# Variances on three partition groups, so that the merge's small matmuls use row groups of TensorE

## The chip, the cores and the metric

The program runs on one core of one Trainium2 chip. The metric is the time of one execution on the device in microseconds (us), the median of several runs.

## The reference, cut to what matters

The input is 8 images of 64 x 64 positions with 96 channels. Four layers follow each other, each adding its result to its input:

```python
x = x + L0(_gn(x), ...)      # cross kind
x = x + L1(_gn(x), ...)      # snake kind
x = x + L2(_gn(x), ...)      # cross kind
x = x + L3(_gn(x), ...)      # causal kind, one direction, no layer norm
```

Inside a layer the channels are projected to 192, convolved and gated, and a state-space recurrence runs over the positions in four directions (in L3 in one). What matters here is how layers 0 to 2 end, for every position, over its 192 channels:

```python
y = out[:, 0] + inv[:, 0] + wh + invwh          # the four directions, plus Ds * xs
mu = y.mean(-1, keepdims=True)
var = y.var(-1, keepdims=True)
y = (y - mu) * rsqrt(var + 1e-05) * ln_gamma + ln_beta
y = y * silu(z)
return y @ out_proj_w.T                          # 192 -> 96
```

## The kernel before

`build` runs, for each of the four layers, `expand_stage`, `scan_stage` and `merge_stage`, one after the other, each as a block with its own program for every engine. The images are worked on in pairs, four pairs in all. The 192 channels of two images are 384 rows, laid on the 128 partitions as three tiles (`TILES`): tile 0 holds the first 128 channels of image 0, tile 2 those of image 1, and tile 1 the last 64 channels of both, image 0 on partitions 0 to 63 and image 1 on 64 to 127. An image has 4,096 positions, worked on in eight banks (`NB`) of 512 columns.

`merge_stage` (lines 1137 to 1505) does two things at once. In each bank of pair p it also takes three of the 24 jobs that sum the directions of pair p + 1: SyncE (SP) loads `ya`, `yb` and, for a row job, `ub` (512 KB each) into one of three slots; GpSimd (POOL) adds ya and yb (`pair_up`, L1483); VectorE (DVE) adds them to `total` (`add_job`: L1427 a row job, L1438 a column job, which in the snake kind is two instructions of half the size). Jobs come as four row jobs and four column jobs, three times over.

The bank itself, in a normalized layer, goes through these steps, with semaphores between the engines:

- `centre` (L1287, TensorE, PE): 7 matmuls of 128 x 128 on 512 columns subtract the mean and leave the centred values in `cent`.
- `square` (L1365) and `take` (L1370, both ScalarE, ACT): the squares go to `sq`, a copy to `tn`.
- `variance` (L1297, PE): 3 matmuls with the 2-column table `average_by` sum the squares of both images into two partitions of `scale[:, 0, :]`.
- `deviation` (L1376, ACT): square root into `root`, 2 partitions by 512.
- reciprocal (L1462, DVE), in place in `root`.
- `spread` (L1305, PE): 3 matmuls, one for each tile, with the 2-row table `spread_by` carry 1/deviation from the two partitions to all 128, into the three banks of `scale`.
- product (L1467, DVE) of `tn` and `scale`; `gain` (L1382, ACT); gate by `zc` (L1504, POOL).
- `project` (PE): for each image b one matmul on the 128 rows of its own tile (L1318) and one on its 64 rows of tile 1 (L1320), added up in bank b of `outp`.
- `residual` (L1209, DVE) adds `outp` to `xr`, which SP loaded (L1258) and stores after the last bank (L1268).

The order is written out by hand. On PE a bank is `variance(c)`, `centre(c + 1)`, `spread(c)`, `project(c - 1)`:

```python
variance(p, c)
if c + 1 < NB:
    centre(p, c + 1, half)
spread(p, c)
if c:
    project(p, c - 1)
```

On DVE it is the reciprocal, one job, the product, the bank's two other jobs, `residual(c - 1)`. On ACT it is the root, `square(c + 1)`, `gain(c)`, `take(c + 1)`. On POOL it is three `pair_up`, then the gate. `variance` waits for the squares and for the product of the bank before; `spread` for the reciprocal; `project` for the gate and for the residual of the bank before it; SP's loads of a job wait until DVE is done with the job three before, and its load of `xr` for the store of the last pair. The causal layer has no variance, no spread and its own branch in `project`.

Of the kernel before, what the change touches and what calls it, by code (L numbers as in the profile page):

```python
# [22 lines left out]
ACT = mybir.ActivationFunctionType  # L23

P = 128
# [1111 lines left out]
def merge_stage(nc, kind, T, W, useq, yseq, zgate, x_t, out, last):  # L1137
# [27 lines left out]
    with ExitStack() as ctx:  # L1165
# [4 lines left out]
        def sb(name, shape, dt=F32):  # L1170
            return ctx.enter_context(nc.sbuf_tensor(name + W["tag"], shape, dt))
# [10 lines left out]
        average_by = sb("average_by", [P, TILES, 2])  # L1182
        spread_by = sb("spread_by", [2, TILES, P])
        zc = [sb(f"zc{j}", [P, TILES, BANK]) for j in range(2)]
        sq = sb("sq", [P, TILES, BANK]) if norm else None
        root = sb("root", [2, BANK])
# [25 lines left out]
        with nc.Block() as block:  # L1212
# [65 lines left out]
            def _(pe):  # L1278
# [13 lines left out]
                def variance(p, c):  # L1292
                    pe.wait_ge(sem["squared"], p * NB + (c + 1))

                    pe.wait_ge(sem["normed"], p * NB + (c + 1))
                    for s in range(TILES):
                        mm = pe.matmul(scale[0:2, 0, :], average_by[:, s, :], sq[:, s, :], start=(s == 0),  # L1297
                                       stop=(s == TILES - 1))
                    mm.then_inc(sem["var_full"], 1)

                def spread(p, c):

                    pe.wait_ge(sem["inverted"], p * NB + (c + 1))
                    for s in range(TILES):
                        mm = pe.matmul(scale[:, s, :], spread_by[:, s, :], root[:, :], start=True, stop=True)  # L1305
                    mm.then_inc(sem["spread"], 1)

                def project(p, c):
# [6 lines left out]
                    for b in range(2):  # L1315
                        rows = slice(64 * b, 64 * b + 64)
                        if not last:
                            pe.matmul(outp[0:DM, b, :], wo[:, 2 * b * DM:(2 * b + 1) * DM], g[:, 2 * b, :],  # L1318
                                      start=True, stop=False)
                            mm = pe.matmul(outp[0:DM, b, :], wo[rows, DM:2 * DM], g[rows, 1, :],  # L1320
                                           start=False, stop=True)
                        else:
# [37 lines left out]
            def _(act):  # L1360
# [11 lines left out]
                def deviation(p, c):  # L1372
# [3 lines left out]
                    act.activation(root[:], scale[0:2, 0, :], ACT.Sqrt, bias=T["eps"][0:2, 0:1])\  # L1376
# [192 lines left out]
def constants():  # L1569
# [9 lines left out]
    for b in range(2):  # L1579
        for n in range(NS):  # L1580
            pick[:, b, n, b, n // QUADS, n % QUADS] = one
    group = np.kron(np.eye(DM // 3), np.ones((3, 3))) / 3
# [5 lines left out]
        "average": (np.stack([batch == 0, batch == 1], axis=-1) / DI).astype(np.float32),  # L1588
        "spread": np.stack([batch.T == 0, batch.T == 1]).astype(np.float32),
# [68 lines left out]
```

## Time and profile before

| | |
|---|---|
| median of 3 runs | 39,340.68 us (39,318.74 to 39,354.67) |
| the profiled execution, its own time | 39,340.42 us |
| its span, first to last instruction | 39,338.6 us |
| mean granted TensorE clock | 0.754 of full speed |
| instructions | 330,119 |

The profile is of one execution. "Busy" is the time an engine spent in instructions; a matmul in f32 is recorded as two passes over its columns, so counts of PE are twice those of the program. PEld is the load of weights, which overlaps PE. The granted clock is 1.00 for 2.4 GHz and 0.50 for 1.2 GHz. In a timeline consecutive instructions of one kind are merged into a row with their count (x14), and the last bracket tells how long the engine had idled and which instruction released it. "Cross", "snake" and "causal" are the kinds of the layers.

### The profile page before, as it was taken

What the parts mean: (1) busy time and instruction counts of PE and PEld (TensorE: products, weight loads), DVE (VectorE), ACT (ScalarE), POOL (GpSimd) and SP (SyncE); (2) the same over time, 40 slices, a digit from 0 to 9 for tenths busy, and PEclk for the clock granted to TensorE, in tenths of its full rate; (3) what the DMA queues carried; (4) which work ended last, traced back from release to release, by engine and by line L of the source; (5) the groups of instructions that cost most, each with busy time, mean ns of one, the idle gap of its engine ahead of it and who ended that gap; (6) DMA issues with size and microseconds to landing.
All of it is one profiled execution on the core that took longest, in us unless ns stands there. A gap on an engine that the chain in (4) does not pass through costs nothing. (4 is left out here: it accounts for less than half of the span.)

```text
span 39338.6 us, 330119 instructions
## 1 busy us (share of the span) xinstructions
PE 27496.9 (70%) x73952; PEld 7178.8 (18%) x73952; DVE 34763.5 (88%) x18992; ACT 18062.4 (46%) x22589; POOL 33220.1 (84%) x7824
## 2 busy tenths in 40 slices
PE   3777777777774777777777774777777777775777
PEld 1111111111111111111111111111111111111114
DVE  6999999999957999999999967999999999965994
ACT  2555555555522554554555522545455454523451
POOL 1999999999962999999999952999999999963994
PEclk6777777777766777777777766777777777777775
DMA  4666666666664666666666664666666666665665
GB/s 132 160 160 157 161 160 161 158 162 160 160 213 146 158 161 159 162 159 159 157 161 161 161 212 145 159 159 157 160 160 159 159 157 160 161 209 162 158 157 174
DMA packets 2388645, 6388.13 MB, mean 162 GB/s; under 512 B 692056, under 2 KB 835936, under 8 KB 2376032
## 3 DMA queue, kind: packets, MB, share of 16 engines
q1 hardware_dynamic: 2387040, 6374.58, 62.7%
q14 instruction: 1556, 12.75, 0.1%
q8 instruction: 49, 0.80, 0.0%
HBM read 2973.68 MB, written 764.47 MB: 95 GB/s over the span
## 5 line engine op out<-in xcount | busy, mean ns | idle before, releaser
L1100 POOL TENSOR_TENSOR h<-h,c 128x2048 f32<-128x2048 f32 x4992 | 22509.1, 4525 | 1278.4 <-ACT state L959 1274.3
L901 DVE TENSOR_TENSOR_SCAN h<-decay,state,slot 128x1024 f32<-128x1024 f32 x6656 | 15615.9, 2346 | 681.1 <-ACT state L1047 20.1
L809 PE MATMUL psy<-h,t_fold 128*32 128x512 f32 x40000 | 12230.6, 787 | 265.6 <-ACT ybuf L1020 265.6
L744 PE MATMUL slot<-bc,pick 96*128 96x512 bf16 x13328 | 5060.7, 477 | 8763.4 <-DVE h L897 5512.5
L877 DVE TENSOR_TENSOR slot<-du,slot 128x1024 f32<-128x1024 f32 x6656 | 8050.7, 1210 | 1039.3 <-PE slot L744 945.0
L951 ACT ACTIVATE decay<-delta,na 128x1024 f32<-128x1024 f32 x6664 | 7583.2, 1146 | 2332.2 <-DVE h L901 2158.6
L897 DVE TENSOR_TENSOR_SCAN h<-slot,state,made 128x1024 f32<-128x1024 f32 x3328 | 7624.6, 2326 | 15.5 <-ACT slot L951 15.5
L1120 POOL TENSOR_TENSOR made<-du,b 128x2048 f32<-128x2048 f32 x1664 | 7524.6, 4522 | 127.1 <-DMA b<-bcdram 123.4
L951 ACT ACTIVATE slot<-delta,na 128x1024 f32<-128x1024 f32 x3328 | 3716.6, 1117 | 6481.4 <-DVE h L901 6476.4
L809 PEld LDWEIGHTS psy<-h,t_fold 128*32 128x32 f32 x40000 | 2244.1, 131 | 8523.9 <-issue 8231.2
L744 PEld LDWEIGHTS slot<-bc,pick 96*128 96x128 bf16 x13328 | 908.9, 104 | 14839.8 <-DVE h L897 8044.3
L959 ACT COPY state<-h 128x2 f32<-128x2 f32 x4992 | 925.8, 185 | 3762.3 <-DVE h L901 2769.4
L1112 POOL TENSOR_TENSOR du<-delta,u 128x1024 f32<-128x1024 f32 x628 | 1483.6, 2362 | 929.0 <-ACT delta L998 929.0
L762 PE MATMUL psc<-dts,wdt 32*128 32x512 f32 x2512 | 1977.6, 893 | 0.9 <-ACT dts L1031 0.9
L441 POOL COPY us<-us 128x4096 f32<-128x4096 f32 (+1 forms) x48 | 359.0, 7494 | 1913.4 <-ACT us L359 1913.4
L1483 POOL TENSOR_TENSOR ya<-ya,yb 128x1024 f32<-128x1024 f32 x360 | 1030.7, 2873 | 793.4 <-DMA ub<-useq 740.2
L777 PE MATMUL psc<-relu,t_ident 128*128 128x512 f32 x2512 | 1658.8, 795 | 22.8 <-DVE excess L908 22.8
L422 DVE SCALAR_TENSOR_TENSOR acc<-xp,convw,acc 128x4096 f32<-128x4096 f32 x312 | 1560.1, 5000 | 11.2
L998 ACT COPY delta<-psc 128x1024 f32<-128x1024 f32 x628 | 635.5, 1012 | 1989.5 <-PE psc L777 1989.5
L752 PE MATMUL psc<-u,wx 128*96 128x512 f32 x2544 | 1482.1, 683 | 30.6 <-DMA bdt<-in_bdt 29.8
L777 PE MATMUL psc<-log,t_ident 128*128 128x512 f32 x2512 | 1326.3, 624 | 0.0
L777 PE MATMUL psc<-excess,t_less 128*128 128x512 f32 x2512 | 1179.7, 592 | 0.0
(103 smaller groups left out, 17260.9 us busy)
## 6 DMA issues: line engine op xcount, KB each, us to landing
delta<-delta SPq DMA_DIRECT2D x10048, 128.0 KB, 2.8
du<-du SPq DMA_DIRECT2D x10048, 128.0 KB, 2.9
c<-bcdram SPq DMA_DIRECT2D x6720, 128.0 KB, 2.8
b<-bcdram SPq DMA_DIRECT2D x6688, 128.0 KB, 3.0
u<-useq SPq DMA_DIRECT2D x212, 1536.0 KB, 6.6
yseq<-ybuf SPq DMA_DIRECT2D x624, 512.0 KB, 2.7
ya<-yseq SPq DMA_DIRECT2D x420, 512.0 KB, 4.3
yb<-yseq SPq DMA_DIRECT2D x360, 512.0 KB, 5.1
```

The lines of the kernel that those rows point to most:

```text
L422: dve.scalar_tensor_tensor(out=a, in0=src, scalar=w, in1=a, op0=ALU.mult, op1=ALU.add).then_inc(sem["conv_step"], 1)
L744: mm = pe.matmul(slot[s % 2][:, cols], pick[:, rows_of, :], bc[q % 2][:, cols], start=True, stop=True)
L762: pe.matmul(psc[:, HALF[a]], wdt[q][:, t, :], dts[q][:, HALF[a]], start=True, stop=True)\
L777: mm = pe.matmul(psc[:, HALF[a]], T["less" if term == 2 else "ident"][:, :], (relu, log, excess)[term][:, HALF[a]], start=(term == 0), sto ...
L809: mm = pe.matmul(psy[rows, cols], T["fold"][:, :], h[v % H_RING][:, c, cols], start=(v % QUADS == 0), stop=(v % QUADS == QUADS - 1), skip_ ...
L877: dve.tensor_tensor(slot[s % 2][:], du4[j % DU_RING][:, s % 2, :], slot[s % 2][:], ALU.mult)\
L897: dve.tensor_tensor_scan(out, slot[s % 2][:, order], made[p % MADE_RING][:, s % 2, order], first, ALU.mult, ALU.add).then_inc(sem["h_ready ...
L901: dve.tensor_tensor_scan(out, decay[s % DECAY_RING][:, order], slot[s % 2][:, order], first, ALU.mult, ALU.add).then_inc(sem["h_ready"], 1)
L951: act.activation(dst[:], delta4[j % DELTA_RING][:, s % 2, :], ACT.Exp, scale=na[q][:, k:k + 1])\
L1100: pool.tensor_tensor(both[:], both[:], c4[g][:].unsqueeze(1).broadcast_to((P, 2, CH)), ALU.mult)\
L1112: pool.tensor_tensor(du[:], delta[:], u[q][:, t, :], ALU.mult).then_inc(sem["du_ready"], 1)
L1120: pool.tensor_tensor(made[k % MADE_RING][:], du4[j % DU_RING][:], b4[k % B_RING][:].unsqueeze(1).broadcast_to((P, 2, CH)), ALU.mult)\
```

## The change

Three tables and the code around them change. `average_by` has 96 columns instead of 2: columns 0 and 1, 32 and 33, 64 and 65 hold the same two averages and the rest are zero, so the variances of the two images come out three times, on partitions 0, 32 and 64. `root` has 96 partitions, and the root and the reciprocal work on all of them. `spread_by` is one table of 96 x 128, in which rows 32s and 32s + 1 serve tile s; the matmul for tile s reads its weights and its moving data from those two partitions. In `project`, outside the last layer, the two matmuls of 128 rows now come first and the two of 64 rows (partitions 0 to 63 and 64 to 127) after them.

```diff
--- before.py
+++ after.py
@@ -1179,11 +1179,12 @@
         dsum = sb("dsum", [P, TILES])
         lng, lnb = (sb(n, [P, TILES]) for n in ("lng", "lnb"))
         centre_by = sb("centre_by", [P, TILES, TILES, P])
-        average_by = sb("average_by", [P, TILES, 2])
-        spread_by = sb("spread_by", [2, TILES, P])
+
+        average_by = sb("average_by", [P, TILES, 96])
+        spread_by = sb("spread_by", [96, P])
         zc = [sb(f"zc{j}", [P, TILES, BANK]) for j in range(2)]
         sq = sb("sq", [P, TILES, BANK]) if norm else None
-        root = sb("root", [2, BANK])
+        root = sb("root", [96, BANK])
         tn = [sb(f"tn{j}", [P, TILES, BANK]) for j in range(2)]
         ob = sb("ob", [P, 2, 4, DM]) if last else None
         cent = ctx.enter_context(nc.psum_tensor("cent" + W["tag"], [P, TILES, BANK], F32))
@@ -1294,15 +1295,17 @@
 
                     pe.wait_ge(sem["normed"], p * NB + (c + 1))
                     for s in range(TILES):
-                        mm = pe.matmul(scale[0:2, 0, :], average_by[:, s, :], sq[:, s, :], start=(s == 0),
+                        mm = pe.matmul(scale[0:96, 0, :], average_by[:, s, :], sq[:, s, :], start=(s == 0),
                                        stop=(s == TILES - 1))
                     mm.then_inc(sem["var_full"], 1)
 
                 def spread(p, c):
 
                     pe.wait_ge(sem["inverted"], p * NB + (c + 1))
+
                     for s in range(TILES):
-                        mm = pe.matmul(scale[:, s, :], spread_by[:, s, :], root[:, :], start=True, stop=True)
+                        rows = slice(32 * s, 32 * s + 2)
+                        mm = pe.matmul(scale[:, s, :], spread_by[rows, :], root[rows, :], start=True, stop=True)
                     mm.then_inc(sem["spread"], 1)
 
                 def project(p, c):
@@ -1312,14 +1315,18 @@
                     if last and c == 0:
                         pe.wait_ge(sem["x_in"], p * 16 + 16)
                     g = tn[c % 2]
-                    for b in range(2):
-                        rows = slice(64 * b, 64 * b + 64)
-                        if not last:
+                    if not last:
+                        for b in range(2):
                             pe.matmul(outp[0:DM, b, :], wo[:, 2 * b * DM:(2 * b + 1) * DM], g[:, 2 * b, :],
                                       start=True, stop=False)
+
+                        for b in range(2):
+                            rows = slice(64 * b, 64 * b + 64)
                             mm = pe.matmul(outp[0:DM, b, :], wo[rows, DM:2 * DM], g[rows, 1, :],
                                            start=False, stop=True)
-                        else:
+                    else:
+                        for b in range(2):
+                            rows = slice(64 * b, 64 * b + 64)
                             for j in range(4):
                                 o = outp[:, b, j * DM:(j + 1) * DM]
                                 tok = slice(j * P, (j + 1) * P)
@@ -1373,7 +1380,7 @@
 
                     act.wait_ge(sem["spread"], p * NB + (c + 1))
                     act.wait_ge(sem["var_full"], p * NB + (c + 2))
-                    act.activation(root[:], scale[0:2, 0, :], ACT.Sqrt, bias=T["eps"][0:2, 0:1])\
+                    act.activation(root[:], scale[0:96, 0, :], ACT.Sqrt, bias=T["eps"][0:96, 0:1])\
                         .then_inc(sem["rooted"], 1)
 
                 def gain(p, c):
@@ -1579,14 +1586,19 @@
     for b in range(2):
         for n in range(NS):
             pick[:, b, n, b, n // QUADS, n % QUADS] = one
+    average, spread = np.zeros((P, TILES, 96)), np.zeros((96, P))
+    for s in range(TILES):
+        for b in range(2):
+            average[:, :, 32 * s + b] = (batch == b) / DI
+            spread[32 * s + b] = batch[:, s] == b
     group = np.kron(np.eye(DM // 3), np.ones((3, 3))) / 3
     return {
         "ident": np.eye(P, dtype=np.float32),
         "pick": pick.reshape(96, 2 * QUADS, P),
         "fold": np.tile(np.eye(GROUP, dtype=np.float32), (QUADS, 1)),
         "group": group.astype(np.float32),
-        "average": (np.stack([batch == 0, batch == 1], axis=-1) / DI).astype(np.float32),
-        "spread": np.stack([batch.T == 0, batch.T == 1]).astype(np.float32),
+        "average": average.astype(np.float32),
+        "spread": spread.astype(np.float32),
         "centre": (eye - same / DI).astype(np.float32),
     }
```

The order of instructions changes on PE alone, in two places. The first is a steady bank of a merge: the spread (L1305 before, L1308 now) and the projection behind it. `outp<-tn_0,wo` is a matmul of the projection. Before:

```order
L1287 MATMUL cent<-total_0,centre_by 128x512 x7
L1305 MATMUL scale<-root,spread_by 128x512 x3
L1318 MATMUL outp<-tn_0,wo 96x512
L1320 MATMUL outp<-tn_0,wo 96x512
L1318 MATMUL outp<-tn_0,wo 96x512
L1320 MATMUL outp<-tn_0,wo 96x512
L1297 MATMUL scale<-sq,average_by 2x512 x3
```

Now:

```order
L1288 MATMUL cent<-total_0,centre_by 128x512 x7
L1308 MATMUL scale<-root,spread_by 128x512 x3
L1320 MATMUL outp<-tn_0,wo 96x512 x2
L1325 MATMUL outp<-tn_0,wo 96x512 x2
L1298 MATMUL scale<-sq,average_by 96x512 x3
```

The matmul of 64 rows of image 0 (L1320 before, L1325 now) has moved behind the matmul of 128 rows of image 1 (L1318 before, L1320 now), and stands next to its twin.

The second is the end of a pair, where two projections follow the last spread (REGISTER_ALU prepares a semaphore's value). Before:

```order
L1305 MATMUL scale<-root,spread_by 128x512 x3
L1309 REGISTER_ALU
L1318 MATMUL outp<-tn_0,wo 96x512
L1320 MATMUL outp<-tn_0,wo 96x512
L1318 MATMUL outp<-tn_0,wo 96x512
L1320 MATMUL outp<-tn_0,wo 96x512
L1309 REGISTER_ALU
L1318 MATMUL outp<-tn_0,wo 96x512
L1320 MATMUL outp<-tn_0,wo 96x512
L1318 MATMUL outp<-tn_0,wo 96x512
L1320 MATMUL outp<-tn_0,wo 96x512
```

Now:

```order
L1308 MATMUL scale<-root,spread_by 128x512 x3
L1312 REGISTER_ALU
L1320 MATMUL outp<-tn_0,wo 96x512 x2
L1325 MATMUL outp<-tn_0,wo 96x512 x2
L1312 REGISTER_ALU
L1320 MATMUL outp<-tn_0,wo 96x512 x2
L1325 MATMUL outp<-tn_0,wo 96x512 x2
```

Both projections are regrouped in the same way; what stands before and behind them is as it was.

## Rows read from the trace of the kernel before

**Rows 1.** The page, part 1: busy us of each engine, share of the span, instructions.
```profile
PE 27496.9 (70%) x73952; PEld 7178.8 (18%) x73952; DVE 34763.5 (88%) x18992; ACT 18062.4 (46%) x22589; POOL 33220.1 (84%) x7824
```

**Rows 2.** Table by stretch: us, each engine's busy time (instructions), clock, DMA share, GB/s.
```profile
11050.00:11980.00 930.00, 701.03 (x1088) 191.61 (x1088) 462.67 (x249) 189.23 (x196) 473.21 (x152) 0.68 0.64 225
22850.00:23800.00 950.00, 701.37 (x1088) 190.94 (x1088) 533.67 (x375) 190.50 (x197) 460.39 (x152) 0.67 0.64 223
```

**Rows 3.** Timeline of PE, one steady bank: start us, us, engine, line, operation.
```profile
11220.50 6.28 PE L1287 MATMUL cent<-total,centre_by 128*128 128x512 f32 x14
11226.70 2.84 PE L1305 MATMUL scale<-root,spread_by 2*128 2x512 f32 x6
11229.47 1.22 PE L1318 MATMUL outp<-tn,wo 128*96 128x512 f32 x2
11230.62 2.02 PE L1320 MATMUL outp<-tn,wo 64*96 64x512 f32 x2
...
11236.48 4.75 PE L1297 MATMUL scale<-sq,average_by 128*2 128x512 f32 x6
```

**Rows 4.** Timeline of DVE: the reciprocals that bound the intervals, one product.
```profile
11200.68 3.34 DVE L1462 RECIPROCAL root<-root 2x512 f32<-2x512 f32 x1 [3.70 <-ACT root L1376]
...
11229.65 1.75 DVE L1467 TENSOR_TENSOR tn<-tn,scale 128x1536 f32<-128x1536 f32 x1 [2.75 <-PE scale L1305]
...
11324.65 3.34 DVE L1462 RECIPROCAL root<-root 2x512 f32<-2x512 f32 x1 [3.48 <-ACT root L1376]
...
11422.70 3.33 DVE L1462 RECIPROCAL root<-root 2x512 f32<-2x512 f32 x1
...
11528.28 3.34 DVE L1462 RECIPROCAL root<-root 2x512 f32<-2x512 f32 x1 [4.63 <-ACT root L1376]
```

**Rows 5.** Table by stretch, columns as in rows 2: granted clock and DMA.
```profile
11220.50:11226.70 6.20, 6.20 (x15) 2.57 (x14) 5.32 (x2) 0.68 (x1) 3.99 (x3) 1.00 0.93 359
11226.70:11229.47 2.77, 2.77 (x7) 1.03 (x6) 0.20 (x1) 1.45 (x1) 2.29 (x1) 1.00 0.51 160
11230.70:11236.40 5.70, 5.70 (x6) 1.10 (x6) 4.19 (x3) 2.23 (x3) 2.57 (x1) 0.50 0.59 201
11236.50:11241.10 4.60, 4.60 (x7) 0.57 (x6) 1.28 (x2) 1.44 (x1) 4.02 (x3) 0.56 1.01 395
11362.30:11365.00 2.70, 2.68 (x7) 0.44 (x7) 0.00 (x0) 1.30 (x1) 0.00 (x0) 1.00 0.59 206
11023.60:11027.30 3.70, 3.68 (x17) 0.64 (x16) 3.60 (x3) 1.09 (x1) 3.70 (x2) 0.50 1.04 240
11168.00:11325.00 157.00, 150.41 (x250) 41.88 (x250) 82.58 (x49) 46.45 (x47) 88.46 (x30) 0.76 0.70 244
```

**Rows 6.** Timeline of the scan before the merge: the fold on PE.
```profile
11023.63 3.66 PE L809 MATMUL psy<-h,t_fold 128*32 128x512 f32 x16
```

**Rows 7.** Groups by line and shape: count, busy us, mean ns, idle before.
```profile
L1438 DVE TENSOR_TENSOR total<-total,ya 128x1024 f32<-128x1024 f32 x120 | 361.2, 3010 | 36.5 <-POOL ya L1483 32.0
L1438 DVE TENSOR_TENSOR total<-total,ya 128x512 f32<-128x512 f32 x120 | 240.4, 2003 | 14.4 <-POOL ya L1483 11.0
L1427 DVE SCALAR_TENSOR_TENSOR total<-ub,dsum,ya 128x1024 f32<-128x1024 f32 x240 | 336.3, 1411 | 864.3 <-DMA ub<-useq 519.2 <-POOL ya L1483 345.2
L1462 DVE RECIPROCAL root<-root 2x512 f32<-2x512 f32 x96 | 320.4, 3338 | 407.1 <-ACT root L1376 407.1
L1209 DVE TENSOR_TENSOR xr<-xr,outp 96x512 f32<-96x512 f32 x128 | 81.7, 676 | 156.7 <-PE outp L1320 156.7
L1320 PEld LDWEIGHTS outp<-tn,wo 64*96 64x96 f32 x384 | 74.7, 254 | 278.7 <-issue 278.7
```

**Rows 8.** Timeline of PE and DVE at the end of the first pair.
```profile
11328.04 5.49 PE L1305 MATMUL scale<-root,spread_by 2*128 2x512 f32 x6 [4.20 <-DVE root L1462]
...
11335.31 7.96 DVE L1438 TENSOR_TENSOR total<-total,ya 128x1024 f32<-128x1024 f32 x2
...
11352.30 8.40 PE L1287 MATMUL cent<-total,centre_by 128*128 128x512 f32 x14
```

## The prediction

> **What bounds it now.** The page first [rows 1]: over the whole run VectorE (DVE) is busy 88%, GpSimd (POOL) 84%, TensorE (PE) 70%. Those shares belong to the scan, which the change leaves alone; only the three normalized merges are touched. A table by stretch [rows 2] shows the first (cross) and the second (snake), 930 and 950 us long: PE is busy 701 us in both, VectorE only 463 and 534, GpSimd 473 and 460. The third is of the first's kind. Together they are about 2,800 us, 7% of the run, and a gain can come from nowhere else.
>
> Next, one steady bank on PE [rows 3]. By the starts, the centring takes 6.20 (11220.50 to 11226.70), the spread 2.77, and the projection of the bank before 7.01: four matmuls, the first 1.15 to the next one's start, so the other three 5.86 / 3 = 1.95 each. VectorE's reciprocals give the beat [rows 4]: six intervals from 11200.68 to 11324.65 are 20.66 us each, and in the second pair five from 11422.70 to 11528.28 are 21.1. The variance is then 20.66 less the other three, 4.68, and nothing is left for a gap on PE. A first pair of a merge has six such intervals and each of the other three has five, 21 per merge, 63 in all. In them PE is the bound.
>
> Then the clock [rows 5]. The centring and the spread are granted 1.00 (2.4 GHz). The clock falls right behind the spread, which streams only 2 of 128 rows for 2.77 us; the rest of the projection is granted 0.50 (1.2 GHz), and so is nearly all of the variance (0.56). It is back when the centring begins, after full-height variances. Where PE went from a centring straight to a variance, that variance had 1.00 and took 2.67 us.
>
> **The change, part by part.** Every f32 matmul is recorded as two passes, so the spread's 3 matmuls are 6 passes (x6 in the row).
>
> 1. *Spread.* Its three matmuls now sit in row groups 0, 32 and 64 and write different banks. No row of the kernel shows row groups side by side. The ends are: nothing gained (6 rounds, 2.77), or all at once (2 rounds, 2.77 - 4 x 0.44 = 1.0; 0.44 is the centring's 6.20 / 14 passes). The nearest row is the scan's fold with 32-column weights in different column groups [rows 6]: 16 passes took 3.66 us while the clock was 0.50 [rows 5], about 0.9 us per round of four; one after another they would take 16 x 0.9 = 14. I take 1.0, saving 1.77.
>
> 2. *Projection.* The two half-height matmuls now follow each other, in rows 0 to 63 and 64 to 127, into different banks. By the same row I let them run together: three steps, not four, saving 1.95 in the low clock; the other end is 0. At full clock a step is at most 1.15 (the first matmul in rows 3), three are 3.45.
>
> The Trainium skill, "TensorE: Matmul & The Clock Gate", in its part on packing small matmuls, says that matmuls start and end strictly in program order. By that rule the second pass of one matmul would hold the next one back: spread 4 rounds, the two halves 3 passes long, 0.9 and 0.9 us dearer. The fold's row speaks against it: in strict order only the second pass of one and the first of the next could overlap, 8 rounds or 7 us, where 3.66 was measured.
>
> 3. *Variance.* 96 weight columns, not 2. A load of 96 columns is 254 ns [rows 7], under the pass before it (0.44 or more). Cost 0; if that cover is gone, 6 x 0.25 = 1.5 us a bank. The pass itself should not change: at full clock one with 2 weight columns (variance, 2.67 / 6) and one with 128 (centring) both take 0.44.
>
> 4. *Square root and reciprocal* take 512 elements per partition on 96 partitions, not 2. VectorE's product on 128 partitions by 1,536 takes 1.75 and the reciprocal on 2 by 512 takes 3.34 [rows 4, 7]: the partitions clearly do not set the time. I count nothing; were the reciprocal half as long again, VectorE's banks would grow by 1.7 and the gain fall by a third. ScalarE (ACT) is busy 46 of 157 us [rows 5] and could take twice the root.
>
> 5. *Loads.* The two tables grow by some 190 KB a merge: 4 merges times 0.5 us at the 359 GB/s of the centring in rows 5, +2 us.
>
> **The steady bank after it.** In the clock as now: 20.66 - 1.77 - 1.95 = 16.9. With the clock high all through: 6.20 + 1.0 + 3.45 + 2.67 = 13.3. I take the clock as mostly high, since what preceded each fall, the long 2-row stretch, shrinks to 1 us and the halves are paired to full height. Then PE is no longer the bound, and others are:
>
> - DMA: busy share 0.70 of 157 us in the first pair's eight banks (the stretch holds 7.6) [rows 5]: 110 / 7.6 = 14.5 us a bank.
> - VectorE: reciprocal 3.34, product 1.75, residual 2 x 0.68, together 6.44, and three jobs: a row job is 1.41, a column job 3.01 in the cross kind and 2 x 2.00 in the snake kind [rows 7]. The five steady banks hold 2, 0, 3, 1, 1 column jobs: cross 13.9, 10.7, 15.5, 12.3, 12.3; snake 15.9, 10.7, 18.5, 13.3, 13.3.
>
> The larger of DMA and VectorE bank by bank averages 14.7 (cross) and 15.6 (snake). To both I add 0.8 for hand-overs (an estimate: four a bank of about 0.2, as from the spread's end at 11229.47 in rows 3 to the product at 11229.65 in rows 4), since these engines now wait for one another. So 15.5 and 16.4, against 20.66: 42 x 5.15 + 21 x 4.25 = 306 us.
>
> **The pair ends.** Here the clock is low and one chain counts [rows 8]: spread at 11328.04 (5.49, 0.9 a pass), product, two jobs that hold VectorE 7.96, residual, last projection, next centring at 11352.30. The spread becomes 1.9 (-3.6) and the projection three steps (-1.95): 5.5 for each of 12 pair ends, 66 us. Between the last reciprocal of this pair and the third of the next lie 98 us in three intervals [rows 4]; behind the pair end they wait for the residual's 3 MB store and load and for jobs. For the last two of them I count 0, and keep 3.5 us each, one low spread (18 of them, 63 us), for the lower end.
>
> **Sum.** 306 + 66 - 2 = 370 us. The profiled execution took 39,340.4 us (span 39,338.6), a hair below the median of 39,340.7: **38,970 us**, 0.94% less. About 0.2% (80 us) is what a measurement of this kernel can tell from no change.
>
> **Rivals.**
>
> *A. The clock keeps its two halves.* For it: the projection and the variance ran low although PE had no gap. Against: the spread before each fall is cut to a third. Interval 16.9 (only the snake's bank of 18.5 is above): 63 x 3.7 + 66 = 299, giving 39,040. Chance 0.18.
>
> *B. Passes in strict order, or no overlap at all.* Strict order at high clock makes the PE bank 13.3 + 1.8 = 15.1, still under 15.5, and a pair end saves 2.8, so 306 + 34: 39,000; with the clock of rival A it is 18.7, 123 + 34: 39,180. No overlap leaves two fewer changes of matmul height a bank, some 0.12 us each (1.95 against 5.49 / 3), 96 x 0.24 = 23: 39,320, no change. Chance 0.06 for strict order, 0.06 for none.
>
> *C. Slower: the clock stays low through the centring.* Row-group matmuls use few rows, and shorter variances leave PE waiting for VectorE, so the clock might not rise before the centring. A bank all low: 2 x 6.20 + 1.9 + 3 x 1.95 + 2 x 2.67 = 25.5, or 4.8 over today; 63 x 4.8 - 66 = 236 slower: 39,580. The sign turns where the bank passes 20.66 by more than a pair end's saving, at about (20.66 - 13.3) / (25.5 - 13.3) = 60% of the way to all low. For: pair ends where the spread ran low throughout. Against: the clock rises today after a variance that ran low. Chance 0.05.
>
> **Numbers.** Forecast 0.65, A 0.18, B 0.12, C 0.05. Low end: no hand-over cost (14.7 and 15.6, 357 us) plus 66 and 63: 486 less, 38,854, taken as 38,840. High end: past A, to strict order in the low clock, cut at 39,150. Left out are no overlap, C and tails. Faster by over 0.2%: 0.65 + 0.18 + 0.06 and a little lost to tails, 0.89; the same 0.06; slower 0.05.
>
> **What would show it.** Right: the spread's six passes take about 1.0 us at full clock, three starts within 0.05 us; the two half-height matmuls start together; the projection takes 3.5 us or less; steady reciprocals stand 14 to 19 us apart, unevenly, longest where three column jobs fall; PE waits for VectorE; granted clock of the first pair's 157 us above 0.76. Wrong: an even beat of 17 (A), six spread passes one by one at 0.44 (B), centrings of 12 us (C), a reciprocal or root that takes longer than 3.34 or 0.8 us, or PE loads that show between the variance's passes.

## The result and the profile after

The changed kernel takes 38,959.85 us (median of 4 runs, 38,956.73 to 39,009.38) against 39,329.71 us before in the same measurement: 370 us less, a ratio of 0.9906 with a 95% interval of [0.9893, 0.9918]. It is faster. The profiled execution of the changed kernel has a span of 38,961.1 us.

The page, part 1, of the changed kernel (busy us, share of the span, instructions), beside [rows 1]:

```profile
PE 26823.7 (69%) x73952; PEld 7089.6 (18%) x73952; DVE 34963.4 (90%) x18992; ACT 18056.2 (46%) x22589; POOL 33194.7 (85%) x7824
```

PE lost 673 us of busy time with the same number of instructions. VectorE gained 200 us, though it was given no more work: its jobs take longer, of which more below.

The timeline of PE in the changed kernel, two banks of the first pair (start us, us, line, operation; compare [rows 3]):

```profile
11247.08 1.75 PE L1308 MATMUL scale<-root,spread_by 2*128 2x512 f32 x6 [2.86 <-DVE root L1469]
11248.76 3.73 PE L1320 MATMUL outp<-tn,wo 128*96 128x512 f32 x4
11252.42 2.01 PE L1325 MATMUL outp<-tn,wo 64*96 64x512 f32 x4
11254.36 2.81 PE L1298 MATMUL scale<-sq,average_by 128*96 128x512 f32 x6
11257.02 6.17 PE L1288 MATMUL cent<-total,centre_by 128*128 128x512 f32 x14
11263.28 1.13 PE L1308 MATMUL scale<-root,spread_by 2*128 2x512 f32 x6
11264.34 1.96 PE L1320 MATMUL outp<-tn,wo 128*96 128x512 f32 x4
11266.23 1.10 PE L1325 MATMUL outp<-tn,wo 64*96 64x512 f32 x4
11267.26 2.81 PE L1298 MATMUL scale<-sq,average_by 128*96 128x512 f32 x6
```

The second bank is the forecast to the letter: the spread's six passes are over in 1.06 us (11263.28 to 11264.34), where [rows 3] had 2.77; the two half-height matmuls (four passes) take 1.03 us, the time of one; projection 2.92 and variance 2.7 (from 4.68), all at full clock. Taken one by one, the first passes of its three spread matmuls start 0.007 us apart (11263.277, .284, .291), and so do the second ones (.811, .817, .824). The first bank is of another kind: PE waited 2.86 us for the reciprocal, and the projection behind it ran low (3.66 and 1.94 us). Both kinds are common. In 33 of the 63 steady banks the projection ran below full clock: in none of the 18 in which PE had waited less than 0.5 us before the spread, in 32 of the 36 in which it had waited over 1.5 us. The table by stretch says the same of the two banks, and gives the first pair's steady banks (us; busy PE, PEld, DVE, ACT, POOL; clock, DMA share, GB/s; for the kernel before see [rows 5]):

```profile
11248.80:11254.30 5.50, 5.50 (x11) 1.32 (x8) 5.40 (x4) 2.23 (x3) 3.57 (x2) 0.50 0.65 245
11263.30:11270.00 6.70, 6.70 (x20) 2.00 (x20) 6.70 (x3) 4.31 (x5) 2.98 (x2) 1.00 0.96 322
11184.00:11293.00 109.00, 90.37 (x222) 31.23 (x220) 99.45 (x47) 39.62 (x42) 82.37 (x26) 0.92 0.82 290
```

For the kernel before, that last stretch reads:

```profile
11184.00:11293.00 109.00, 106.99 (x184) 30.34 (x182) 66.75 (x36) 32.09 (x33) 62.37 (x20) 0.78 0.69 242
```

PE was full (107 of 109 us) and is not any more; the clock went from 0.78 to 0.92. (A fixed stretch catches other banks in each execution: the changed kernel's second profile has 0.86 in the same one. Over all 63 steady intervals the two profiles agree, 0.901 and 0.906, against 0.725 before.)

The reciprocals on VectorE after the change, answering to [rows 4]: six intervals from the first of these rows to the second, five from the third to the fourth.

```profile
11194.75 3.35 DVE L1469 RECIPROCAL root<-root 96x512 f32<-96x512 f32 x1 [3.04 <-ACT root L1383]
...
11293.05 3.34 DVE L1469 RECIPROCAL root<-root 96x512 f32<-96x512 f32 x1
...
11384.12 3.33 DVE L1469 RECIPROCAL root<-root 96x512 f32<-96x512 f32 x1
...
11461.43 3.33 DVE L1469 RECIPROCAL root<-root 96x512 f32<-96x512 f32 x1
```

That is 16.4 and 15.5 us an interval, from 20.66 and 21.1. They are uneven, from 11.6 to 19.9 us in the cross kind.

**Where the 370 us are.** The starts of all 96 reciprocals, the first centrings and the ends of the last residuals divide the three merges completely (us, profiled executions):

| part | before | after | saved |
|---|---|---|---|
| 42 steady intervals, cross | 20.89 each | 15.72 each | 217 |
| 21 steady intervals, snake | 20.94 each | 17.16 each | 79 |
| 9 crossings from pair to pair, 3 intervals each | 98.9 each | 95.2 each | 34 |
| 3 ends, last reciprocal to last residual | 28.8 each | 24.1 each | 14 |
| 3 starts, first centring to second reciprocal | 32.6 each | 29.7 each | 9 |
| together, first centring to last residual | 2,391.8 | 2,038.4 | 353 |

The spans differ by 377.5; 24 us lie outside the merges, and no run here says where they come from. A second profile of the changed kernel (last experiment) has a span 51 us longer than the first while its merges are 11 us shorter, so that much moves from one execution to another.

### The profile page after: what moved, and what is told of

Its sections match the earlier page's. It is cut to its first block and busy times, and to the rows that moved or that the text cites. A ratio compares the mean times of both kernels' runs of the same rounds, so it can differ in the third digit from the quotient of the medians.

```text
span 38961.1 us, 330119 instructions
## 1 busy us (share of the span) xinstructions
PE 26823.7 (69%) x73952; PEld 7089.6 (18%) x73952; DVE 34963.4 (90%) x18992; ACT 18056.2 (46%) x22589; POOL 33194.7 (85%) x7824
## 5 line engine op out<-in xcount | busy, mean ns | idle before, releaser
L897 DVE TENSOR_TENSOR_SCAN h<-slot,state,made 128x1024 f32<-128x1024 f32 x3328 | 7625.6, 2326 | 17.4 <-ACT slot L951 17.4
L1434 DVE SCALAR_TENSOR_TENSOR total<-ub,dsum,ya 128x1024 f32<-128x1024 f32 x240 | 483.1, 2018 | 905.7 <-DMA ub<-useq 519.5
```

Source lines behind the costliest of these rows:

```text
L897: dve.tensor_tensor_scan(out, slot[s % 2][:, order], made[p % MADE_RING][:, s % 2, order], first, ALU.mult, ALU.add).then_inc(sem["h_ready ...
```

## The experiments

Each kernel is compared with the kernel before on the same chip. "Interval" is the mean of the 42 (cross) and 21 (snake) steady intervals, got from the profile's reciprocals as above; "clock" is the mean granted clock over these 63 intervals.

| kernel | time | before | ratio, 95% | interval cross, snake | clock | three merges |
|---|---|---|---|---|---|---|
| before | | | | 20.89, 20.94 | 0.725 | 2,391.8 |
| changed | 38,959.9 | 39,329.7 | 0.9906 [0.9893, 0.9918] | 15.72, 17.16 | 0.901 | 2,038.4 |
| spread only | 39,072.6 | 39,353.3 | 0.9928 [0.9911, 0.9944] | 16.35, 17.99 | 0.854 | 2,113.7 |
| projection only | 39,077.8 | 39,353.3 | 0.9929 [0.9912, 0.9945] | 16.13, 18.20 | 0.880 | 2,104.8 |
| 96 rows, no overlap | 39,068.6 | 39,353.3 | 0.9928 [0.9911, 0.9944] | 15.88, 17.65 | 0.960 | 2,105.1 |
| 2 rows, no overlap | 39,363.0 | 39,365.7 | 0.9999 [0.9990, 1.0009] | 20.66, 20.90 | 0.728 | 2,378.7 |
| changed, 32 rows a group | 38,994.3 | 39,353.3 | 0.9909 [0.9893, 0.9926] | 15.91, 16.94 | 0.905 | 2,035.0 |

### The clock by itself

Is the gain that of matmuls running side by side, or that of the clock? Two kernels have the passes of the kernel before, one after the other, and the wider tables of the change. Between the two only the line with `rows` differs; against the changed kernel the first edits the spread like this:

```diff
-                        rows = slice(32 * s, 32 * s + 2)
-                        mm = pe.matmul(scale[:, s, :], spread_by[rows, :], root[rows, :], start=True, stop=True)
+                        rows = slice(0, 96)
+                        mm = pe.matmul(scale[:, s, :], spread_by[rows, s, :], root[rows, :], start=True, stop=True)
```

The control, named "2 rows, no overlap" in the table, has `rows = slice(0, 2)`. Both have a `spread_by` of 96 x 3 x 128, zero in all rows but the first two, and the old order in `project`.

> The passes of the kernel before, one after the other and in its order, but the spread streams 96 rows instead of 2 (zero weights in all rows but the first two; root and reciprocal on 96 partitions). No overlap of row groups at all. Theory 1 (rows streamed decide the clock): the spread stays at 2.77 us but the clock no longer falls behind it; projection about 4 x 1.03 and variance 2.67 at full clock, the PE bank about 15.8 us, the intervals about 16.5 (cross) and 17.5 (snake), the time 39,330 - 250, about 39,080. Theory 2 (the clock falls for another reason, such as waits or weight columns): interval 20.66 and no change, 39,330.

> The tables, the root and the reciprocal of the change (96 weight columns in the variance, 96 partitions), but the spread's three matmuls all read rows 0 and 1 and the projection keeps its old order: the kernel of the run with 96 rows, with 2 rows streamed instead. If the wider tables cost and give nothing and rows streamed decide the clock: spread 2.77 us, the clock falls behind it, interval 20.66 to 20.9, time within 0.1% of 39,350. If 96 weight columns in the variance are what lifts the clock, it is as fast as the run with 96 rows, 39,070.

With 96 rows the kernel takes 285 us less than the one before; with 2 rows it takes the same (ratio 0.9999). The timeline of PE with 96 rows:

```profile
11255.74 2.84 PE L1308 MATMUL scale<-root,spread_by 96*128 96x512 f32 x6 [0.62 <-DVE root L1465]
11258.42 1.02 PE L1321 MATMUL outp<-tn,wo 128*96 128x512 f32 x2
11259.37 1.10 PE L1323 MATMUL outp<-tn,wo 64*96 64x512 f32 x2
11260.40 1.10 PE L1321 MATMUL outp<-tn,wo 128*96 128x512 f32 x2
11261.42 1.10 PE L1323 MATMUL outp<-tn,wo 64*96 64x512 f32 x2
11262.45 2.81 PE L1298 MATMUL scale<-sq,average_by 128*96 128x512 f32 x6
11265.10 6.17 PE L1288 MATMUL cent<-total,centre_by 128*128 128x512 f32 x14
```

and with 2:

```profile
11254.89 2.84 PE L1308 MATMUL scale<-root,spread_by 2*128 2x512 f32 x6
11257.65 1.10 PE L1321 MATMUL outp<-tn,wo 128*96 128x512 f32 x2
11258.68 2.02 PE L1323 MATMUL outp<-tn,wo 64*96 64x512 f32 x2
11260.63 2.02 PE L1321 MATMUL outp<-tn,wo 128*96 128x512 f32 x2
11262.58 2.02 PE L1323 MATMUL outp<-tn,wo 64*96 64x512 f32 x2
11264.53 4.99 PE L1298 MATMUL scale<-sq,average_by 128*96 128x512 f32 x6
11269.36 6.17 PE L1288 MATMUL cent<-total,centre_by 128*128 128x512 f32 x14
```

The spread takes 2.7 us in both. Behind 96 rows the projection takes 4.0 us and the variance 2.65; behind 2 rows 6.9 and 4.8. The table by stretch has the clock (columns as above), of the projection with 96 rows and then of its last three quarters with 2:

```profile
11258.42:11262.45 4.03, 4.03 (x9) 0.89 (x8) 3.76 (x3) 1.98 (x3) 2.35 (x1) 1.00 0.98 367
11258.70:11264.53 5.83, 5.83 (x7) 1.16 (x7) 3.28 (x3) 2.22 (x3) 2.61 (x1) 0.50 0.69 254
```

So two things are shown: in this order of matmuls the rows that the spread uses decide whether the clock (1.00 or 0.50) stays up behind it, and this alone, with no overlap anywhere, is worth three quarters of what the change brings (285 of 370 us). The one line changes the rows of the weights together with the moving rows; which of the two counts was not separated. And the other novelties, 96 weight columns in the variance and root and reciprocal on 96 partitions, cost nothing that can be measured: the reciprocal is 3.34 us in both kernels, a root 0.68.

### Each half of the change alone

Spread only: the changed kernel with the old `project`. Projection only: the kernel before with this edit.

```diff
-                    for b in range(2):
-                        rows = slice(64 * b, 64 * b + 64)
-                        if not last:
+                    if not last:
+                        for b in range(2):
                             pe.matmul(outp[0:DM, b, :], wo[:, 2 * b * DM:(2 * b + 1) * DM], g[:, 2 * b, :],
                                       start=True, stop=False)
+
+                        for b in range(2):
+                            rows = slice(64 * b, 64 * b + 64)
                             mm = pe.matmul(outp[0:DM, b, :], wo[rows, DM:2 * DM], g[rows, 1, :],
                                            start=False, stop=True)
...
```

> Only the spread runs in three row groups; the projection keeps its old order (128, 64, 128, 64 rows). Theory 1, the long stretch of 2 rows is what lets the clock fall: the spread takes 1.06 us as in the changed kernel, the clock stays high through projection and variance in most steady banks, the PE bank is about 14.4 us and the intervals about 16 (cross) and 17.3 (snake); with 3.6 us at each of 12 pair ends the time is 39,330 - 290 - 43, about 39,000, nearly the whole gain. Theory 2, the half-height matmuls of the projection keep the clock low: the projection still takes 1.95 us a matmul, the interval is an even 18.9 us, and the time is 39,330 - 63 x 1.77 - 43, about 39,175.

> Only the order in the projection changes (the two matmuls of 64 rows stand next to each other); variances on two partitions and the spread of 2 rows as before, 2.77 us. Theory 1 (the spread lets the clock fall): the clock still falls behind every spread, the projection is 3 steps of 1.95, the interval is 18.7 us, and the time is 39,330 - 63 x 1.95 - 12 x 1.95, about 39,185. Theory 2 (the half heights keep it low): the paired halves count as full height, the clock comes back within the projection, the interval is under 17.5 us and the time under 39,120.

They save 281 and 276 us, and together they would make 557, where the change brings 370. The first came out between the two theories, nearer the first (333 expected, 155 by the rival). The second refutes "the spread alone decides" (in the cross kind the interval is under the 17.5 us of its theory 2, in the snake kind, with 18.20, it is not). In some banks the clock does fall behind the spread of 2 rows but comes back within the paired projection, in time for the variance; in others it does not fall at all. This timeline of the projection-only kernel has one of each:

```profile
11255.09 2.84 PE L1305 MATMUL scale<-root,spread_by 2*128 2x512 f32 x6 [1.13 <-DVE root L1466]
11257.86 3.10 PE L1317 MATMUL outp<-tn,wo 128*96 128x512 f32 x4
11260.89 1.60 PE L1322 MATMUL outp<-tn,wo 64*96 64x512 f32 x4
11262.42 2.74 PE L1297 MATMUL scale<-sq,average_by 128*2 128x512 f32 x6
...
11271.30 2.84 PE L1305 MATMUL scale<-root,spread_by 2*128 2x512 f32 x6
11274.06 1.96 PE L1317 MATMUL outp<-tn,wo 128*96 128x512 f32 x4
11275.95 1.10 PE L1322 MATMUL outp<-tn,wo 64*96 64x512 f32 x4
```

In the first the variance takes 2.67 us to the next start, not 4.68. Of the 45 steady banks of this kernel in which PE did not wait before the spread, 22 kept the full clock through the projection; in the kernel before it was none of 54. So both stretches of few rows had to do with the low clock, and mending either brings most of it back. That is one reason why the two savings do not add up; a likely second, since the intervals of all three kernels lie near 16 us in the cross kind, is that PE is no longer the bound there.

### More rows on top of the change

```diff
-                        rows = slice(32 * s, 32 * s + 2)
+                        rows = slice(32 * s, 32 * s + 32)
```

> The changed kernel, but each of the three spread matmuls streams all 32 rows of its row group (zero weights in 30 of them). Theory 1 (rows streamed decide the clock): granted clock in the steady banks rises from 0.91 to 0.93 towards 1.00; since PE is no longer the bound there, the time falls by 0 to 30 us below 38,960. Theory 2: clock and time as in the changed kernel.

A miss on the clock: it is 0.905 in the steady intervals, where the changed kernel has 0.901 and 0.906 in its two profiles, and ratio (0.9909) and merges (2,035) are those of the change. The low stretches that are left stand behind PE's waits for the reciprocal here too: the projection ran low in none of the 19 steady banks with a wait under 0.5 us and in 31 of the 40 with one over 1.5. More rows in a spread of 1 us do not help there.

### What bounds a steady bank now

My sum had put the larger of VectorE's own work and 14.5 us of DMA there, plus 0.8 us of hand-overs. In a steady stretch of the changed kernel's second pair, 77 us long (11384 to 11461), GpSimd's rows (count, busy us, mean ns, idle before) are:

```profile
L1490 POOL TENSOR_TENSOR ya<-ya,yb 128x1024 f32<-128x1024 f32 x15 | 44.7, 2988 | 12.9 <-DMA ub<-useq 10.3 <-DMA yb<-yseq 2.6
L1511 POOL TENSOR_TENSOR tn<-tn,zc 128x1536 f32<-128x1536 f32 x5 | 19.9, 3989 | 5.3 <-ACT tn L1389 5.3
```

and VectorE's:

```profile
L1434 DVE SCALAR_TENSOR_TENSOR total<-ub,dsum,ya 128x1024 f32<-128x1024 f32 x8 | 24.3, 3044 | 2.3 <-POOL ya L1490 2.3
L1445 DVE TENSOR_TENSOR total<-total,ya 128x1024 f32<-128x1024 f32 x7 | 20.5, 2925 | 0.2
```

A row job, 1.41 us in [rows 7], takes 3.04 here. The timeline shows how: one that starts at 11411.29, just as GpSimd begins a gate of 3.44 us at 11411.20, ends after 4.43 us.

```profile
11411.20 3.44 POOL L1511 TENSOR_TENSOR tn<-tn,zc 128x1536 f32<-128x1536 f32 x1
11411.29 4.43 DVE L1434 SCALAR_TENSOR_TENSOR total<-ub,dsum,ya 128x1024 f32<-128x1024 f32 x1 [2.26 <-POOL ya L1490]
```

Six kernels asked which of GpSimd, VectorE, the loads and the number of slots sets the pace. The first five ran once each, so their totals are rough (39,366 or, for the two without ub, 39,327 us is the kernel before); the intervals carry the argument.

| kernel | time | interval cross, snake |
|---|---|---|
| GpSimd adds 32 of 1,024 columns | 38,716 | 13.71, 14.79 |
| no yb loaded | 38,798 | 13.87, 15.69 |
| reciprocal on 128 of 512 columns | 38,947 | 15.52, 16.90 |
| no ub loaded, 3 slots | 38,863 | 14.38, 16.08 |
| no ub loaded, 4 slots | 38,890 | 14.40, 16.04 |
| gate on VectorE (5 rounds) | 38,912.9 | 15.82, 16.81 |

```diff
-                    pool.tensor_tensor(ya[s][:], ya[s][:], yb[s][:], ALU.add).then_inc(sem["paired"], 1)
+                    pool.tensor_tensor(ya[s][:, 0:32], ya[s][:, 0:32], yb[s][:, 0:32], ALU.add).then_inc(sem["paired"], 1)
```

> The changed kernel, but GpSimd adds ya and yb on 32 of 1,024 columns only (the rest of yb is left out of the sum); all loads and all of VectorE's work stay. Theory L (VectorE's jobs and GpSimd's additions hold each other up, so that their times add: 3 x 2.35 + 3.42 + 3 jobs of 1.27 or 2.27 are about 15.8 us a bank in the cross kind): the jobs fall back to 1.28 and 2.3 us and the intervals to 14.0 or less (cross) and 15 (snake), which is PE's or VectorE's own sum. Theory D (DMA, 14.5 us a bank, is the bound): intervals stay at 14.5 to 15.7 in the cross kind.

```diff
...
-                    if K > 1:
-
-                        sp.dma_start(yb[s][:], y_v[first + 2, pair, c, t]).then_inc(job_in[s], 16)
...
-                    pool.tensor_tensor(ya[s][:], ya[s][:], yb[s][:], ALU.add).then_inc(sem["paired"], 1)
+                    pool.tensor_tensor(ya[s][:], ya[s][:], ya[s][:], ALU.add).then_inc(sem["paired"], 1)
```

> The changed kernel, but yb is not loaded and GpSimd adds ya to itself (one of two directions is left out): 24 x 512 KB less of a pair's 42 MB, some 30%, with GpSimd's and VectorE's work as it was. Theory L: steady intervals stay near 15.7 (cross) and 17.2 (snake). Theory D: they fall by up to 30%, to the PE bank of about 13.5.

```diff
-                                dve.reciprocal(root[:], root[:]).then_inc(sem["inverted"], 1)
+                                dve.reciprocal(root[:, 0:128], root[:, 0:128]).then_inc(sem["inverted"], 1)
```

> The changed kernel, but the reciprocal works on 128 of 512 columns (the others keep the deviation), about 1.0 us instead of 3.34. If VectorE's own work is the bound of a steady bank, as I put it in the prediction, the intervals fall by about 2.3 us, to 13.4 (cross) and 14.9 (snake). If GpSimd or DMA is the bound, by less than 1 us.

With all of the traffic but little of GpSimd's additions, the interval is 13.7 us: 14.5 us of DMA a bank was no floor. VectorE's jobs are short again, though nothing was done to them; over the whole run a row job takes 1.41 us and a column job 2.89, where the changed kernel has 2.02 and 3.53:

```profile
L1434 DVE SCALAR_TENSOR_TENSOR total<-ub,dsum,ya 128x1024 f32<-128x1024 f32 x240 | 338.5, 1414 | 862.3 <-DMA ub<-useq 516.8 <-POOL ya L1490 339.2 <-POOL tn L1511 4.8
L1445 DVE TENSOR_TENSOR total<-total,ya 128x1024 f32<-128x1024 f32 x120 | 347.2, 2893 | 16.4 <-POOL ya L1490 13.0
```

Without yb the interval falls as well, to 13.9, which the theory of the two engines alone had not expected. That run changes two things, though: adding ya to itself takes GpSimd 2.35 us instead of 2.82, and for three additions a bank that comes to 1.4 us, of the 1.85 gained. The run without ub (3 slots, below) is the cleaner one on the loads: its additions are as long as ever (2.84), and the interval is 14.4.

And 2.4 us less work for VectorE brings 0.2. Of the 230 us that the reciprocals lose in the merges, the jobs take back some 70 in longer durations and 100 in waits for ya. The groups by line of that run:

```profile
L1469 DVE RECIPROCAL root<-root 96x128 f32<-96x128 f32 x96 | 90.0, 938 | 165.7 <-ACT root L1383 165.7
L1445 DVE TENSOR_TENSOR total<-total,ya 128x1024 f32<-128x1024 f32 x120 | 487.8, 4065 | 55.3 <-POOL ya L1490 48.4
```

A column job there is 4.07 us, where the changed kernel has 3.53. So VectorE's own work, which I had named, was not the bound. GpSimd's row fills the 77 us: 58.8 of work inside the stretch (the first and last instruction of the groups above reach over its edges), 12.9 of waiting for loads and 5.3 for the gain. Shorter additions shorten the interval, and so do fewer loads. That GpSimd's row sets the pace is the reading that fits these runs; it is not settled, as the gate will show.

Would a fourth slot for loads help? The two runs without ub make room for it. They leave the input's share of the sum out (a row job reads ya twice). The edit of the run with four slots, cut to what matters; the one with three has all but its first two lines:

```diff
-    DEPTH = 3
+    DEPTH = 4
...
-        yb = [sb(f"yb{j}", [P, CH]) for j in range(DEPTH)]
-        ub = [sb(f"ub{j}", [P, CH]) for j in range(DEPTH)]
+        second = [sb(f"yb{j}", [P, CH]) for j in range(DEPTH)]
+        yb, ub = (second, ya) if K > 1 else (ya, second)
...
-                    if w == "row":
+                    if w == "row" and K == 1:
                         sp.dma_start(ub[s][:], u_v[0, pair, c, t]).then_inc(job_in[s], 16)
```

> Control for the next run: the changed kernel without the loads of ub in the normalized merges (a row job reads ya twice, so the input's share Ds x u of the sum is left out); three slots as before. 12 x 512 KB less a pair, some 15% of its loads. Row jobs land sooner; steady intervals about 15 (cross) and 16.5 (snake), between the changed kernel (15.7 and 17.2) and the run without yb (13.9 and 15.7).

> As the control, with four slots for jobs instead of three. Theory S (the round trip of a slot is the bound: a slot serves one job a bank, and its load, GpSimd's addition, VectorE's job and the waits between them add up to the interval): with four slots a round trip may last 1.33 intervals, so the steady intervals fall by 1 us or more below the control, towards PE's own 13.5 (cross), and uneven banks are evened out. Theory L (VectorE's jobs and GpSimd's additions hold each other up) or D (DMA rate): intervals as in the control, within 0.4 us.

14.40 against 14.38: without ub, the round trip of a slot is not the bound. With ub it was not tried. Last, the gate (tn x zc) moved from GpSimd to VectorE, with the changed kernel again beside it:

```diff
-                            for j in now:
+                            for n, j in enumerate(now):
                                 add_job(p + 1, j)
+                                if norm and n == 0:
+                                    dve.wait_ge(sem["affine"], p * (TILES * NB) + TILES * (c + 1))
+                                    dve.wait_ge(gate_in[c % 2], p * (8 * NB) + 16 * (c // 2 + 1))
+                                    dve.tensor_tensor(tn[c % 2][:], tn[c % 2][:], zc[c % 2][:], ALU.mult)\
+                                        .then_inc(sem["gated"], 1)
...
-                                pool.wait_ge(sem["affine"], p * (TILES * NB) + TILES * (c + 1))
-                                src = tn[c % 2][:]
+                                continue
```

> The changed kernel with the gate (tn x zc) of the normalized merges moved from GpSimd to VectorE, after the bank's second job. Theory G (GpSimd's sequence with its waits for loads is what fills a steady bank after the change: 58.8 us of work, 12.9 of waits for loads and 5.3 for the gain in 77 us): GpSimd loses 3.4 to 3.9 us a bank, VectorE gains about 1.8, and the intervals fall to about 14.3 (cross) and 16 (snake), some 60 to 90 us less than the changed kernel. Theory V (VectorE's own instructions are the bound, as in my prediction): the intervals grow by about 1.8 us, some 110 us more.

> The changed kernel once more, beside the run before it on the same chip: 370 us under the kernel before (ratio 0.9906), steady intervals 15.7 and 17.2.

The changed kernel came out as before: 39,000 us, ratio 0.9907 [0.9891, 0.9924], intervals 15.66 and 17.04, merges 2,027.2. With the gate on VectorE: 38,913 us, ratio 0.9885 [0.9868, 0.9901], intervals 15.82 and 16.81, merges 2,002.5. Both theories missed the intervals: they neither fell to 14.3 nor grew by 1.8. So to relieve GpSimd at VectorE's cost does not shorten a steady bank. The stretch of 77 us shows GpSimd relieved and VectorE nearly full:

```profile
11384.00:11461.00 77.00, 64.12 (x151) 22.91 (x152) 70.86 (x40) 26.86 (x29) 45.45 (x16) 0.87 0.86 314
```

GpSimd works 45.5 us instead of 58.8, VectorE still 70.9, so in this version it takes GpSimd's place. Of the 87 us by which this version lies under the changed kernel, the merges account for 25, mostly in the crossings from pair to pair (92.1 each, from 94.4); the rest is not explained. The intervals of the two ratios overlap, so that it beats the changed kernel is likely but not settled; that it beats the kernel before is.

## Why the prediction was right

Forecast 38,970 us (370 less than the profiled execution before), measured 38,959.85; the range, 38,840 to 39,150, holds it. By its steps:

1. *Spread, 1.77 us saved.* Right where the clock is full: 1.06 us, forecast 1.0; 2.02 at the pair end, forecast 1.9. The mean over the 63 steady banks is 1.31.
2. *Projection, one of four steps saved.* Right: the two halves take the 1.03 us of one. The mean projection is 4.13 us, since it ran low in half of the banks; at full clock it is 2.92, forecast 3.45 at most. Strict order of passes (rival B) is refuted by the same rows: it would have made four rounds of the spread, 1.8 us. Two numbers of that rival were off: counted as the spread is, the fold's eight matmuls would take at least 9 rounds in strict order, 8.1 us, where I had 8 rounds and 7 us; and the 0.9 us for the two halves is the price at low clock, at full clock it is 0.5, so that PE's bank would have been 14.7 us, not 15.1. Neither changes the forecast. The Trainium skill, "TensorE: Matmul & The Clock Gate", in its part on packing small matmuls, also says that matmuls in different row groups overlap; these rows agree with that part, though not with what strict order of the two passes of each matmul would have given. Whole matmuls do keep their order, by the starts given above (0.007 us apart); it is their passes that interleave.
3. *Variance, root, reciprocal, loads at nothing.* Right: with these novelties alone the ratio is 0.9999.
4. *The clock.* Taken as mostly high: 0.901 instead of 0.725 in the steady intervals. Full clock all through, as in the 13.3 us of the sum, it was only where PE had hardly waited. Rival A (it keeps its halves, 16.9 us, an even beat) and rival C (it stays low) did not happen. The reason was right in kind: few rows streamed behind each fall. The weight that I gave to it was too small, though. The sum is written as if the overlap made the gain and the clock let it through, and the run with 96 rows shows that the clock alone, with no overlap, makes 285 of some 370 us.
5. *The steady interval, 15.5 and 16.4.* Measured 15.72 and 17.16; 297 us saved, forecast 306. The size was right, cross nearly exactly, and the reason was wrong. The shape was right too: the third of the five steady intervals of a pair, with its three column jobs, is the longest (17.4 us on average in the cross kind, 21.3 in the snake kind). DMA's 14.5 us was no floor (13.7 measured with the same traffic), and VectorE's own work did not set the pace (2.4 us less of it gave 0.2). I had taken the durations of VectorE's jobs from the trace of before, where GpSimd had pauses; with shorter banks they grew (row job 1.41 to 2.02, column job 3.01 to 3.53 on average), and GpSimd's work with its waits for loads filled the bank. My 0.8 us of hand-overs stood in for that, by luck. What sets the pace now stays open in part: shorter additions and fewer loads shorten the bank, less work for VectorE alone hardly does (0.2 us), and less for GpSimd at VectorE's cost does not.
6. *Pair ends, 5.5 us each, 66 in all.* The same chain now reads:

```profile
11296.44 2.08 PE L1308 MATMUL scale<-root,spread_by 2*128 2x512 f32 x6 [10.41 <-DVE root L1469]
11298.46 3.73 PE L1320 MATMUL outp<-tn,wo 128*96 128x512 f32 x4
11302.12 1.10 PE L1325 MATMUL outp<-tn,wo 64*96 64x512 f32 x4
11309.54 3.30 PE L1320 MATMUL outp<-tn,wo 128*96 128x512 f32 x4 [6.33 <-DVE xr L1210]
11312.78 1.10 PE L1325 MATMUL outp<-tn,wo 64*96 64x512 f32 x4
11313.81 2.41 PE L1288 MATMUL cent<-total,centre_by 128*128 128x512 f32 x5
```

   From spread to centring 17.4 us instead of 24.3 [rows 8], more than forecast, since part of it ran high. But over the whole crossing of three intervals only 3.8 us were kept (98.9 to 95.2), and 4.7 at a merge's end: 48 us, not 66. The first of the three intervals is 6.0 us shorter (42.8 to 36.8), as forecast; the second grew by 2.1 (25.3 to 27.4), the third by 0.1. That it is the loads behind the pair end which took them back is likely, not shown. 9 us at the starts, not in the sum, and the 24 us outside the merges made up for it.

So the total agrees to 10 us because errors of 10 to 25 us in opposite directions met. That is luck: two profiled executions of the changed kernel differ by 51 us. The range was the honest part.

## What to carry to other kernels

Where TensorE is the bound and its clock falls in every round, look at what it streams just before: a matmul with 2 rows on a 128-row array may cost little itself and still halve the pace of what follows. Giving that matmul more rows, with zero weights, is a remedy that needs no row groups (here it took the wider tables, at no measurable cost), and row groups can be worth more than their own passes. And when a change removes the bound, do not take the other engines' times from the old trace as they stand: VectorE's instructions stretched when they began to meet GpSimd's (row job 1.41 to 2.02 us).

## What the runs showed of the hardware

- f32 matmuls whose rows lie in different row groups and whose results go to different banks run side by side, both passes of each: three of 2 rows in 1.06 us, two of 64 rows in 1.03 us at full clock, where one of 64 rows takes 1.03.
- The granted clock behind the spread hung on the rows used in it: 6 passes of 96 rows kept 1.00 and 6 of 2 rows in the same 2.7 us were followed by 0.50, with PE working on without a gap behind it in both. What followed counted too: with the two half-height matmuls side by side, 22 of 45 projections behind such a spread of 2 rows kept 1.00.
- The spread of 96 rows takes no longer than one of 2 rows (2.68 and 2.76 us), and the reciprocal on 96 partitions no longer than on 2 (3.34).
- A VectorE operation with both inputs in SBUF that begins while GpSimd works on its own two-input operation can be held up until that is over: the one shown took 4.43 us beside a gate of 3.44 and ended 1.08 us after it, where the shortest of its kind near it took 1.27 in all. Meanwhile reciprocals beside GpSimd's additions stayed at 3.34. With GpSimd's additions cut to 32 columns, row jobs went from 2.02 back to 1.41 us on average.
